# The B, C and step projection of a Mamba front stage: from plain fp32 products to one fp32r block of both weight parts

## What is computed

```python
xn = _layernorm(x, gamma, beta)                      # 256 wide
x_inner, z = jnp.split(xn @ W_in, 2, axis=-1)        # 512 each
xc = causal depthwise conv of 4 taps(x_inner) + conv_b
x_conv = jax.nn.silu(xc)
xp = x_conv @ W_x                                    # 512 -> 33
Bmat, Cmat = xp[:, :, :16], xp[:, :, 16:32]
delta = jax.nn.softplus(xp[:, :, -1:])
y = _selective_scan(x_conv, A, Bmat, Cmat, delta)
y = (y + x_conv * D_skip) * jax.nn.silu(z)
return y @ W_out + residual
```

## Time and profile before

| | |
|---|---|
| median of 3 runs | 1928.68 us (1924.13 to 1934.57) |
| profiled execution | 1931.31 us, span 1929.5 us |
| stage 1 | from about 17 to 278 us of the span |
| stage 2 | from about 289 to 555 us |
| busy, share of the span | PE 92%, PEld 75%, DVE 56%, ACT 39%, POOL 37% |
| mean granted TensorE clock | 0.963 |

### The profile page before, as it was taken

The page is one execution under the profiler, slowest core; times in us unless marked ns, Lnnn a source line. Parts: engine busy times, 40 slices in busy tenths (PEclk is TensorE's granted clock), DMA queues, the critical chain, the costliest instruction groups (busy, mean ns, idle before and its releaser), DMA issues.

```text
span 1929.5 us, 33493 instructions
## 1 busy us (share of the span) xinstructions
PE 1773.1 (92%) x9010; PEld 1445.7 (75%) x9011; DVE 1076.5 (56%) x2541; ACT 759.0 (39%) x1358; POOL 709.1 (37%) x624
## 2 busy tenths in 40 slices
PE   6999987999947899999999979999999999999980
PEld 4666656888836778888888857888888888888870
DVE  6777757888825666676666653333333333333325
ACT  5777754665522322223232232323333333333226
POOL 1111005999822334445354451323323323223233
PEclk9999998999977999999999999999999999999995
DMA  3444475777623332221122252333333333333329
GB/s 134 170 169 169 169 237 149 249 257 238 232 100 124 104 107 90 77 87 68 73 84 78 78 199 64 54 53 52 53 52 53 53 51 53 53 50 54 53 37 351
DMA packets 137993, 220.91 MB, mean 114 GB/s; under 512 B 40576, under 2 KB 110656, under 8 KB 129616
## 3 DMA queue, kind: packets, MB, share of 16 engines
q1 hardware_dynamic: 112208, 184.58, 29.0%
q0 software_dynamic: 25728, 35.67, 10.8%
HBM read 122.93 MB, written 97.26 MB: 114 GB/s over the span
## 4 chain that ended last, share of the span: by engine, by line
PE 53%; POOL 5%; issue 4%; DMA 3%; DVE 3%; ACT 2%; SPq 0%; POOLq 0%; ACTq 0%; DVEq 0%
PE back_ps L2370 19%; PE back_ps L2388 12%; PE back_ps L2274 5%; POOL back_turned_qk L1655 4%; PE back_ps L2379 3%; PE back_ps L2260 3%; PE back_ps L2251 3%; POOL sorted L1643 2%; PE back_ps L2205 2%; ACT back_out L1808 2%; PE back_ps L2360 2%; PE back_ps L2213 2%; PE back_ps L2170 1%; PE back_ps L2158 1%; DMA back_raw<-in_up_w 1%
## 5 line engine op out<-in xcount | busy, mean ns | idle before, releaser
L2370 PE MATMUL back_ps<-back_w_gu,back_xe_T 128*128 x1632 | 411.0, 400 | 0.9 <-DVE back_xe_T L2105 0.8
L1681 POOL DMA_INDIRECT acc<-back_y,back_token x136 | 211.7, 1557 | 513.1 <-DVE back_y L2127 469.4
L2370 PEld LDWEIGHTS back_ps<-back_w_gu,back_xe_T 128*128 128x128 f32 x1632 | 297.4, 189 | 60.1 <-issue 1.4
L2120 DVE TENSOR_TENSOR back_h<-back_silu,back_ps 128x512 f32<-128x512 f32 x136 | 93.5, 687 | 370.1 <-PE back_ps L2370 370.1
L2388 PE MATMUL back_ps<-back_w_down,back_he_T 128*128 x1088 | 257.4, 379 | 0.8 <-ACT back_he_T L1802 0.8
L2388 PEld LDWEIGHTS back_ps<-back_w_down,back_he_T 128*128 128x128 f32 x1088 | 196.1, 190 | 22.1 <-issue 1.0
L1147 PE MATMUL front_ps<-front_xn_T,front_w_in_parts 128*128 128x512 f32 x768 | 187.2, 400 | 5.2 <-issue 3.3
L1147 PEld LDWEIGHTS front_ps<-front_xn_T,front_w_in_parts 128*128 128x128 f32 x768 | 143.7, 190 | 48.7 <-issue 18.5
L1643 POOL DMA_INDIRECT sorted<-back_x,back_slot x128 | 130.5, 1020 | 134.9 <-DVE back_slot L1952 100.8
L1802 ACT ACTIVATE back_he_T<-back_ps 128x512 f32<-128x512 f32 x136 | 81.4, 598 | 245.0 <-PE back_ps L2379 245.0
L993 DVE SCALAR_TENSOR_TENSOR front_conv<-front_ps,front_conv_wb,front_conv 128x508 f32<-128x508 f32 (+2 forms) x192 | 141.2, 742 | 63.9 <-ACT front_conv L829 59.3
(11 more groups left out here) (222 smaller groups left out, 2897.6 us busy)
## 6 DMA issues: line engine op xcount, KB each, us to landing
back_xe<-sorted SPq DMA_DIRECT2D x136, 136.0 KB, 2.1
gate_T<-front_gate_T SPq DMA_DIRECT2D x16, 1024.0 KB, 4.7
xc_T<-front_xc_T SPq DMA_DIRECT2D x16, 1024.0 KB, 5.6
front_xc_in<-xc_T SPq DMA_DIRECT2D x16, 1024.0 KB, 5.3
front_gate_in<-gate_T SPq DMA_DIRECT2D x16, 1024.0 KB, 6.4
front_x_rows<-in_x SPq DMA_DIRECT2D x16, 512.0 KB, 5.2
front_c_rep<-c_parts SPq DMA_DIRECT2D x128, 64.0 KB, 4.3
front_rows_in<-in_x SPq DMA_DIRECT2D x16, 512.0 KB, 7.3
```

The source lines that it names most:

```text
L1681: pool.indirect_dma_start(out=d["acc"][:, :], out_offset=bass.IndirectOffsetOnAxis(ap=token[:, r:r + 1], axis=0), in_=y[:, r % 2], in_offs ...
L2370: op = nc.tensor.matmul(dst[:, r % 2], xe_T[:, r % 2, x_part, k], w_gu[:, bass.ds(e, 1), m, w_part, k], start=(n == 0), stop=(n == len(PAS ...
```

## The change

Both operands of the projection are now split into a rounded fp32r part and its rest. The two weight parts stand side by side in one stationary block of 97 columns (33, a gap up to 64, and 33 more), made once by DVE (`split_w_x`). The rounded activations (ACT, `round_xc`) and their rests (POOL, `rest_of_xc`) are moved through it one after the other, so PSUM rows 0 to 32 hold the sum with the rounded weights and rows 64 to 96 the sum with the weights' rest. ACT copies rows 64 to 96 out, and DVE adds the two (`join_xp`). The activation parts have two buffers, by the parity of j. The four blocks are no longer in one place: products of blocks 2 and 3 of g-1 follow `project(g, 0)` and `turn(g+1)`, those of blocks 0 and 1 of g follow `project(g, 2)` and `project(g, 3)`. `turn_xp` moves between the halves of `project(g, 3)`, and the last group's evacuation, turn and softplus move behind the first step of stage 2.

```diff
 # POOL
+            def rest_of_xc(g, u, j):
+                pool.wait_ge(xc_high_ready, KI * g + j + 1)
+                nc.gpsimd.tensor_tensor(xc_parts[:, j % 2, 1], xc_T[:, u, j], xc_parts[:, j % 2, 0].bitcast(F32),
+                                        ALU.subtract).then_inc(xc_low_ready, 1)
...
                 for u in range(2):
+                    g = 2 * pair + u
+                    if not is_at(g, 0):
+                        rest_of_xc(g - 1, 1 - u, KI - 1)
+                    rest_of_xc(g, u, 0)
                     if not last:
-                        rstd_of(2 * pair + u + 2, u)
+                        rstd_of(g + 2, u)
+                    rest_of_xc(g, u, 1)
+                    rest_of_xc(g, u, 2)
 # ACT
+            def round_xc(g, u, j):
+                act.wait_ge(xc_ready, KI * g + j + 1)
+                if not (is_at(g, 0) and j < 2):
+                    act.wait_ge(xp_part_done, KI * g + j - 1)
+                nc.scalar.activation(xc_parts[:, j % 2, 0], xc_T[:, u, j], ACT.Copy).then_inc(xc_high_ready, 1)
+
+            def evacuate_xp(g):
+                act.wait_ge(xp_part_done, KI * (g + 1))
+                if not is_at(g, 0):
+                    act.wait_ge(xp_T_ready, g)
+                nc.scalar.activation(xp_low, ps_xp[XP_LOW:XP_BOTH], ACT.Copy).then_inc(xp_low_ready, 1)
...
                     gate(g, u, 0)
+                    if not is_at(g, 0):
+                        round_xc(g - 1, 1 - u, KI - 1)
                     bias_tap(g, u, 1)
                     silu_conv(g, u, 0)
                     gate(g, u, 1)
+                    round_xc(g, u, 0)
                     if ahead:
                         evacuate_turned(g + 1)
                     if not is_at(g, 0):
-                        evacuate_xp(g - 1, 1 - u)
+                        evacuate_xp(g - 1)
                     bias_tap(g, u, 2)
                     silu_conv(g, u, 1)
                     gate(g, u, 2)
+                    round_xc(g, u, 1)
+                    bias_tap(g, u, 3)
+                    silu_conv(g, u, 2)
                     if not is_at(g, 0):
                         evacuate_xp_rows(g - 1)
-                    bias_tap(g, u, 3)
-                    silu_conv(g, u, 2)
                     gate(g, u, 3)
+                    round_xc(g, u, 2)
...
             silu_conv(GROUPS - 1, 1, KI - 1)
+            round_xc(GROUPS - 1, 1, KI - 1)
...
-            evacuate_xp(GROUPS - 1, 1)
-            evacuate_xp_rows(GROUPS - 1)
-            act.wait_ge(xp_rows_ready, GROUPS)
-            softplus_exp(most, every)
+            evacuate_xp(GROUPS - 1)
...
                 if is_at(k, -2):
                     segments(0, most)
+                    evacuate_xp_rows(GROUPS - 1)
+                    act.wait_ge(xp_rows_ready, GROUPS)
+                    softplus_exp(most, every)
 # DVE
+            def split_w_x():
+                gap = XP_LOW - XP
+                nc.vector.tensor_copy(w_x_parts[:, :, 0:XP], w_x).then_inc(w_x_ready, 1)
+                nc.vector.tensor_copy(w_x_parts[:, :, XP:XP_LOW], w_x[:, :, 0:gap]).then_inc(w_x_ready, 1)
+                dve.wait_ge(w_x_ready, 1)
+                nc.vector.tensor_tensor(w_x_parts[:, :, XP_LOW:], w_x, w_x_parts[:, :, 0:XP].bitcast(F32),
+                                        ALU.subtract).then_inc(w_x_ready, 1)
+
+            def join_xp(g, u):
+                dve.wait_ge(xp_low_ready, g + 1)
+                dve.wait_ge(xp_stored[u], loads(g, u, 32) - 16)
+                if not early_group(g):
+                    dve.wait_ge(xp_turned, g - 1)
+                nc.vector.tensor_tensor(xp_T[:, u], ps_xp[0:XP], xp_low, ALU.add).then_inc(xp_T_ready, 1)
...
                     if not (last and u):
                         split(g + 1, 1 - u)
+                    if not is_at(g, 0):
+                        join_xp(g - 1, 1 - u)
                     if not last:
                         statistics(g + 2, u)
...
             all_steps(0, most)
+            join_xp(GROUPS - 1, 1)
             choose()
 # TensorE
-            def project_xp(g, u):
-                if not is_at(g, 0):
+            def project_xp(g, j):
+                pe.wait_ge(xc_low_ready, KI * g + j + 1)
+                if is_at(g, 0) and j == 0:
+                    pe.wait_ge(w_x_ready, 3)
+                elif j == 0:
                     pe.wait_ge(xp_T_ready, g)
-                for j in range(KI):
-                    pe.wait_ge(xc_ready, KI * g + j + 1)
-                    op = nc.tensor.matmul(ps_xp, w_x[:, j], xc_T[:, u, j], start=(j == 0), stop=(j == KI - 1))
-                op.then_inc(xp_done, 1)
+                for part in range(2):
+                    op = nc.tensor.matmul(ps_xp, w_x_parts[:, j], xc_parts[:, j % 2, part], start=(j == 0 and part == 0),
+                                          stop=(j == KI - 1 and part == 1))
+                op.then_inc(xp_part_done, 1)
...
                     project(g, u, 0)
+                    if not is_at(g, 0):
+                        project_xp(g - 1, 2)
                     project(g, u, 1)
                     if not (last and u):
                         turn(g + 1, 1 - u)
                     if not is_at(g, 0):
-                        project_xp(g - 1, 1 - u)
+                        project_xp(g - 1, 3)
                     project(g, u, 2)
-                    if not is_at(g, 0):
-                        turn_xp(g - 1, 1 - u)
-                    project(g, u, 3)
+                    project_xp(g, 0)
+                    project(g, u, 3, None if is_at(g, 0) else lambda: turn_xp(g - 1, 1 - u))
+                    project_xp(g, 1)
...
                 if is_at(k, -2):
                     pe.wait_ge(steps_ready, 1)
                     segments((0, SEQS // 2), (SEQS // 2, most))
+                    turn_xp(GROUPS - 1, 1)
...
                     if is_at(g, 0):
+                        pe.wait_ge(xp_rows_ready, GROUPS)
                         count_rows()
```

More of the change, by code:

```diff
@@ L422 @@
 FRONT_AT = 16640
+XP_LOW = 64
+XP_BOTH = XP_LOW + XP
 def decoder_front(nc, d, same_rows):
@@ L470, in decoder_front @@
         w_x = at("w_x", 193.5, [P, KI, XP])
+        w_x_parts = at("w_x_parts", 190.5, [P, KI, XP_BOTH], F32R)
+        xc_parts = at("xc_parts", 172, [P, 2, 2, GT], F32R)
+        xp_low = at("xp_low", 180, [XP, GT])
         delta = at("delta", 194.25, [P, SEQS])
@@ L501, in decoder_front @@
         ps = ps_of("ps", [P, 8, 512], F32)
-        ps_turn, ps_inner, ps_gate, ps_xp = ps[:, 0:2], ps[:, 2:4], ps[:, 4:6], ps[0:XP, 6]
+        ps_turn, ps_inner, ps_gate, ps_xp = ps[:, 0:2], ps[:, 2:4], ps[:, 4:6], ps[0:XP_BOTH, 6]
         ps_xp_rows = ps[:, 7, 0:GS * XP].rearrange("p (s c) -> p s c", s=GS)
@@ L533, in decoder_front @@
         xc_ready = sem("xc_ready")
-        xp_done = sem("xp_done")
+        w_x_ready = sem("w_x_ready")
+        xc_high_ready = sem("xc_high_ready")
+        xc_low_ready = sem("xc_low_ready")
+        xp_part_done = sem("xp_part_done")
+        xp_low_ready = sem("xp_low_ready")
         xp_T_ready = sem("xp_T_ready")
@@ L763, in body @@
                 for u in range(2):
+                    g = 2 * pair + u
+                    if not is_at(g, 0):
+                        rest_of_xc(g - 1, 1 - u, KI - 1)
+                    rest_of_xc(g, u, 0)
                     if not last:
-                        rstd_of(2 * pair + u + 2, u)
+                        rstd_of(g + 2, u)
+                    rest_of_xc(g, u, 1)
+                    rest_of_xc(g, u, 2)
             in_pairs(pool, body)
+            rest_of_xc(GROUPS - 1, 1, KI - 1)
             def step(k, u):
@@ L843, in silu_conv @@
                     if not early_group(g):
-                        act.wait_ge(xp_done, g - 1)
+                        act.wait_ge(xc_low_ready, KI * (g - 1))
                 nc.scalar.activation(xc_T[:, u, j], conv[:, u, j], ACT.Silu).then_inc(xc_ready, 1)
[L847 to L850, removed]
+            def round_xc(g, u, j):
[8 more added lines that the diff above has]
+                nc.scalar.activation(xp_low, ps_xp[XP_LOW:XP_BOTH], ACT.Copy).then_inc(xp_low_ready, 1)
             def evacuate_xp_rows(g):
@@ L1012, in _ @@
             split(0, 0)
+            split_w_x()
             def body(pair, last):
@@ L1140, in turn, with project @@
                 op.then_inc(turned, 1)
-            def project(g, u, j):
+            def project(g, u, j, between=None):
                 for first, dst, free, per, done in ((j, ps_inner, tap_done, TAPS, inner_done),
@@ L1149, in project @@
                     op.then_inc(done, 1)
-            def project_xp(g, u):
-                if not is_at(g, 0):
+                    if between:
+                        between()
+                        between = None
+            def project_xp(g, j):
[3 more added lines that the diff above has]
+                elif j == 0:
                     pe.wait_ge(xp_T_ready, g)
-                for j in range(KI):
```

(20 more changed lines are left out.)

## The result

| | before | changed |
|---|---|---|
| median | 1930.47 us (4 runs, 1924.13 to 1934.57) | 1945.57 us (4 runs, 1942.20 to 1946.36) |
| ratio | | 1.008, 95% interval 1.0059 to 1.0100 |
| profiled execution, span | 1931.31, 1929.5 us | 1942.20, 1940.5 us |
| beat of stage 1 | 16.15 us | 16.95 us |
| first L1091, now L1144 (scan of group 0) | 296.4 us | 311.9 us |

The change made the kernel 15.1 us slower, 0.8%. The forecast was 1947 in a range of 1937 to 1963. It was built on +18.3 over the 1928.68 that the front shows; a fourth run moved the median of before to 1930.47, and the time lies so near 1947 partly because of that. Lines have moved: the product L1156 is now L1214, the projections L1147 L1200, the turns of x L1139 L1192, the small turns L1165 L1224, the casts and subtractions of the split L1034 and L1037, `rstd_of` L759 to L766.

A forecast was written before the change was run, and what follows sets the result against it. TensorE's queue alone set the 16.15 us beat; a new wait loop would make it 17.25. 14 x 1.1 = 15.4, with the end of stage 1 +16, plus 1.9, gave +18: 1949 profiled, 1947 as median, range 1937 to 1963.

The forecast's parts named there:

- The ring: Stage 1 wait loop over TensorE, ACT, DVE and POOL, closed by POOL's order: beat 17.25 us instead of 16.15.
- The rival that TensorE's own sum of 14.4 sets the beat: Stage 1: TensorE still sets the beat, 14 x 1.75 = 24.5 us less, total 1906; chance 7%.
- step 8: TensorE's product (g,1), after which the next group begins: 0.45 us, bringing the loop to 17.25.
- The lock: POOL's rest (g,0) holds DVE's cast and subtract of the split; without it the loop is 0.3 us shorter.
- TensorE's saving: L1156 removed, 3.55 us a group, 8 fp32r products added, 1.80: TensorE's own sum falls 1.75 to 14.4.
- my figure of 28 us in all: Total of TensorE's product records: some 28 us for 128, at about 0.4 pipelined.
- The ends: Last groups of stage 1 and passage to stage 2: stage 1 ends 16 us later, then 1.9 more.
- SP's interval: Gate store of group 13 to release of silu (15,0) in group 14's DMA wait: stays 25.4 us.
- The release: Freeing of silu (15,0) from its DMA wait near the end of stage 1: about 14.6 us late.
- The sum: Whole kernel: +18 us by the start of stage 2, later stages untouched.
- The clock rival: TensorE idles 2.85 of 17.25 us and its clock falls to 0.80: +28 us, 1975; chance 10%.
- the sign named for it: A TensorE clock under 1.00 before 290 us would show the forecast wrong.

The follow-up runs named there:

- run 1: Changed kernel with POOL making the rest of block 1 ahead of `rstd_of`: 1936.46 us, ratio 1.002 to the kernel before, beat 16.29.
- run 2: Changed kernel with ACT's rounding of block 0 moved behind the evacuations: 1946.06 us, ratio 1.0063 to the kernel before, beat 16.72.
- run 4: Changed kernel with the rest of block 0 made for only 4 of 512 columns, except in the first group: 1943.73 us, ratio 1.0061.
- run 8: Changed kernel with DVE making the statistics of g+2 before the join of g-1: 1980.6 us, ratio 1.0245, beat 19.5 on average.
- run 3: Changed kernel with rest (g,1) ahead of `rstd_of` on POOL and block 0's rounding behind the evacuations on ACT: 1933.82 us, ratio 1.0005.
- run 11: Kernel before the change, with only the `xc` store ahead of SP's 25 loads in the last two groups: 1928.80 us, ratio 0.9999.
- run 10: run 9's kernel with only the `xc` store ahead of SP's 25 loads in the last two groups: 1922.23 us, ratio 0.996.
- run 9: run 3's kernel with the last group's join, turn, rows and softplus put ahead of the first step of stage 2: 1931.06 us, ratio 1.0001.

## Why the prediction came out, point by point

The ring, with each term as predicted and as read from the rows above:

| step | predicted | measured |
|---|---|---|
| 1: first projection to bias tap of block 1 | 4.96 | 5.00 (170.53 to 175.53) |
| 2: tap, three taps of block 1 | 3.10 | 3.19 (158.71 to 161.90) |
| 3: split, with lock | 2.64 | 2.42 (to 164.32) |
| 4: join | 0.69 | 0.61 (to 164.93) |
| 5: statistics | 1.93 | 1.92 (to 166.85) |
| 6: to POOL, rstd and shift | 2.10 | 2.04 (to 168.89) |
| 7: rest (g,1) | 1.38 | 1.33 (to 170.22) |
| 8: product to the next first projection | 0.45 | 0.31 (to 170.53) |
| sum | 17.25 | 16.82 |

The measured parts add up to the 16.82 between two bias taps by the way they are read; what they test is each step.

- **That a ring over POOL's order sets the beat** is shown by run 1: exchanging two calls takes 9.1 us off, more than half of the loss, with the same work on every engine. The rival that TensorE's own sum of 14.4 sets the beat is refuted by the idle time of the changed kernel, and run 1 shows that it doesn't even when POOL's order is mended.
- **The ring's size** was over by 0.43: steps 3 and 8, by 0.22 and 0.14, are the mis-sized terms, with 0.08 in the join. DVE started statistics 0.61 after the join's start although the join is 0.67 long, and the next projection's weights followed 0.31 after the product's start. The turns go by 16.82 and about 17.04 in turn, mean 16.95. The rows place the extra 0.2 of every second group in step 8: there the next projection's weights follow 0.59 after the product's (153.18 to 153.77) and not 0.31. Two groups share one pass of the loop, and the trace has a compare-and-branch of 0.21 on TensorE's queue at 153.28, between the two. In run 1, where this product hardly waits, the turns go by 16.27 to 16.31 without alternation. That the branch is the cause is likely by this, but no run took it out.
- **The lock** is real, and its sign came otherwise than named: the first cast did not start when the rest (g,0) ended (162.58) but was recorded from 161.90 and ended 0.28 behind it. It was also priced too high. The two casts took 1.29 against 0.83, the first 958 ns long where an undisturbed one takes 428, while a rest ran from 161.28 to 162.58. The Trainium skill, page "SBUF — State Buffer", section "SBUF: two separate sides", says that a DVE operation in a two-port mode or with two SBUF inputs and a GpSimd operation exclude each other for a whole instruction. These rows agree with it, as does run 2, where POOL's rest was the one held. But runs 2 and 4 give 0.2 a group for its hold on the casts and not 0.3: without it the second cast waits 0.24 for ACT. One wait stood in front of the other.
- **TensorE's saving**: the pace of two products in 0.45 is borne out (a pair at 156.43 and the next weights at 156.90), my figure of 28 us in all is not. The trace gives 44.9 us of busy time for 128: each pair shows as 0.63 to 0.71, since the records overlap with what follows. A sum of busy time was the wrong test to name.
- **The ends.** SP's interval held: 25.5 from gate store to release, 25.4 before. The release came 10.5 later, not 14.6, because the ring was shorter (14 x 0.80 = 11.2). Behind it I had +1.4; it was +3.0 (last taps end 9.97 after the silu, 6.96 before). That term was the furthest off: the chain of silu, rounding and rest was in the sum, but not that TensorE's idle 3.50 would be followed by a lower clock, and the six projections and what follows at half pace. A further 0.8 was in no term: before, the last silu started 0.03 after the last taps had ended, and now 0.79, since the gate of block 3 (waiting for TensorE) and a rounding stand ahead of it on ACT. From the last silu to the first scan it was 20.6 against 19.4, +1.2 for my 1.9.
- **The sum** at the start of stage 2 was +15.5 for +18, and at its end +16.7. The misses partly cancelled, which is luck: the ring gave 4 less than forecast, the end of stage 1 some 2.4 more, the tail 0.7 less. The profiled execution's span grew by only 11.0, since its back part, which the change leaves alone, took 1366.5 and not 1372.3. In the thirteen profiles here that part takes between 1366.5 and 1375.7. The medians, +15.1, agree with the front part.
- **The rivals.** The clock rival did not happen in the steady groups (1.00 in 150 to 200), though the sign named for it, a clock under 1.00 before 290, did show in two places: in the second group, where rest (g,1) behind `rstd_of` left TensorE idle for 2.68 (0.57 from 33 to 37), and in the last (0.50 from 283 to 289). Exchanging two DVE calls brings it into the steady groups: run 8, at 1980.6. I had weighed it by TensorE's share of idle time. The recorded shares are close (busy 17.14 of 20.17 us in run 8, 43.76 of 50 in the changed kernel), but in run 8 they count products at the lower clock as longer. What differs plainly in the rows is the longest idle piece, 3.06 against 1.07; no run changed the one and kept the other.

**Where the gain of 1.75 a group went.** It is there as less work on TensorE: in run 3 the engine is busy in 46.34 of 50 us, 14.6 of each 15.79. POOL's order puts 0.66 on the beat, ACT's order and the lock together 0.50 more, and at 15.79 a further wait of 1.23 stands, for the rest (g,0); that one is read from the rows of run 3 alone. What is left, 0.36, was then taken by SP's fixed interval and the longer end and tail of stage 1, and shows in the total only once the `xc` store goes first.

## What to carry to other kernels

When work is moved onto an idle engine, look at what already stands in that engine's queue: POOL had been busy in 4.98 of 50 us and still came to set the beat, since an operation that others need at once stood behind one that waits. Draw the loop from one start of the beat to the next, with every hand-off, before trusting the sum of an engine, and then look for the next loop under it (here 16.95, 16.29, 15.79). A wait that costs nothing while TensorE has work queued (run 11) costs at least its full length once TensorE waits for what is behind it (run 10: a wait of 6.7 gone, the first scan 9.2 earlier than in run 9). Of the stores that stand behind a batch of loads, move up only the one whose data is ready early.

## What was not expected of the hardware

- One idle piece of TensorE was enough for the lower clock: 3.50 was followed by 0.50 from 283 to 289 and 3.06 by 0.83 to 0.91 over a group in run 8, with six projections in 2.76 and 2.31 instead of 1.55; 2.68 was followed by 0.57 from 33 to 37. Two pieces of about 1.05 in each group (changed kernel) and one of 1.56 (run 1) left it at 1.00. The length of the piece alone doesn't decide: one of 3.31 at the program's start (13.46 to 16.77) was not followed by a lower clock, 1.00 from 13 to 20.
- The lock works both ways: POOL's rest took 1.57 instead of 1.29 in run 2, when it began (163.07) inside the split's subtraction, and 1.58 in run 3.
- A store that stands behind a batch of loads pays twice: the `xc` store of the last groups was issued late and took 11.8 to land (268.65 to 280.5), against a median of 5.0 over the stage.
- A compare-and-branch takes 0.21 on TensorE's queue and about 0.05 on those of ACT, DVE and POOL.
- An operation of 4 columns on DVE (L1092 at 305.21) took 1.41 while POOL's L800 ran; in the earlier trace rows the same kind took 1.94.
